# Transformer pair with batch attention and experts: the pace of the last groups' scatters, and the place of one ranking product

## The chip, the cores and the metric

The kernel runs on one core of one Trainium2 chip, as one launch. The metric is device time in microseconds (us) for the whole program, the median of several runs. The core's engines are TensorE (PE, with its weight loads shown apart as PEld), VectorE (DVE), ScalarE (ACT), GpSimd (POOL) and SyncE (SP, which issues DMAs); each works through its own queue in order, and the queues are tied together by semaphores.

## The reference

Two layers run over x of shape (16, 512, 128). Each layer normalises, mixes and adds back twice. Layer 0 has causal linear attention and a token-shift FFN; layer 1 has retention and then what this change touches: an attention over the **batch** axis and a mixture of eight experts.

```python
def _mha(x, Wqkv, bqkv, Wo, bo):         # x is (S, B, 128): every attention is over only 16 rows
    S, B, _ = x.shape
    qkv = x @ Wqkv.T + bqkv
    q, k, v = jnp.split(qkv, 3, axis=-1)
    to_heads = lambda t: t.reshape(S, B, H, hd).transpose(1, 2, 0, 3)
    q, k, v = (to_heads(q), to_heads(k), to_heads(v))
    att = jax.nn.softmax(jnp.einsum('bhqd,bhkd->bhqk', q, k) * (1.0 / np.sqrt(hd)), axis=-1)
    o = jnp.einsum('bhqk,bhkd->bhqd', att, v).transpose(2, 0, 1, 3).reshape(S, B, D)
    return o @ Wo.T + bo
def _moe(x, Wg, W1, b1, W2, b2):
    idx = jnp.argmax(xf @ Wg.T, axis=-1)
    for e in range(E):
        m = (idx == e)[:, None].astype(xf.dtype)
        h = jax.nn.relu(xf @ W1[e] + b1[e])
        out = out + m * (h @ W2[e] + b2[e])
y = _layer_norm(x + _mha(x, ...), g1, be1)
z = _layer_norm(y + _moe(y, ...), g2, be2)
```

Each of the 8192 tokens goes to one expert only, so the kernel sorts tokens by expert in a DRAM buffer `ys` and computes each expert's rows once.

## The kernel before

The program is a chain of blocks, each ended by a barrier over all engines. The last two matter here. `attend_and_route` computes the batch attention, the router's logits and each token's place in `ys`, and scatters the tokens there. `run_experts` reads `ys` in 71 slots of 128 rows, applies the expert of each slot and scatters the result to the output. It cannot begin before the barrier at the end of `attend_and_route` (the `with nc.Block()` whose exits are charged to line 1651).

`attend_and_route` handles G = 16 groups of four 128-token tiles as a software pipeline. `run` walks s from -4 to 20, and each engine has a step function that does its part for several groups: `pe_step`, `act_step`, `vec_step`, `pool_step`, `sp_step`. In step s, for a group in the range 0 to 15:

- TensorE: scores(s), q/k/v of group s+2, values(s-1) (`pe_values`, L1388), the transpose of group s+3, and the output product out(s-1) (`pe_out`, L1405, which raises the semaphore `w_ps`). Each operation waits for the operands that ScalarE, VectorE or a DMA make.
- VectorE: vec_u(s-2) (L1414, residual into the row buffer `S`), logits and statistics of it, the maximum and shift of scores(s) (L1334, L1339), the rest of the softmax and a transpose (L1369) whose result SP copies into the tile `ax` by four DMAs (L1377); values(s) waits for these.
- Routing goes by units: pairs of groups for units 0 to 6 (groups 0 and 1, ..., 12 and 13), then group 14 alone (unit 7) and group 15 alone (unit 8). For a unit r, `vec_choose(r)` (L1459 to L1468) picks each token's expert and ends in a prefix scan; `pe_rank(r)` (L1478, L1479) counts tokens ahead of each one; `vec_dest(r)` (L1485 to L1494) turns this into row numbers in `dest`, by a cast on L1492, and carries the counts on to the next unit.
- GpSimd: `pool_row(g, t)` (L1512) scatters tile t of group g into `ys` by an indirect DMA of 128 rows. Group s-5 is scattered in step s. Row t = 0 waits until the unit's `dest` and the group's row contents are there.

What spaces the scatters: up to step 11, GpSimd's own arithmetic for later groups stands between them. From step 12 on (s >= G - 4) that arithmetic has run out but for one addition, and `pool_step` holds the rows of a group back by hand: row 1 after scores(s) (`s_ps`), row 2 after values(s-1) (`o_ps`), row 3 after out(s-1) (`w_ps`), each capped at the last group that exists. After the last scatter, `clear_semaphores` clears unused semaphores, and GpSimd waits until all scatters have landed (`rows_out`). VectorE meanwhile computes the slot tables from the last unit, and SP and ScalarE write eight padding tiles into `ys` (`write_pad`, L1499).

Of the kernel before, what the change touches and what calls it, by code (L numbers as in the profile page):

```python
# [1127 lines left out]
def attend_and_route(nc, A, K, slot_row, expert):  # L1128
# [6 lines left out]
    G = NT // 4  # L1135
    left = sorted(set(nc.released_uncleared_semaphores) - set(K.cleared))
    UG, RG, VG = 7, 6, 5
    with ExitStack() as ctx:
# [380 lines left out]
        def there(g):  # L1519
            return 0 <= g < G  # L1520


        def pe_step(pe, s):
            if there(s):
                pe_scores(pe, s)
            if there(s + 2):
                pe_qk(pe, s + 2)
                pe_v(pe, s + 2)
            if there(s - 1):
                pe_values(pe, s - 1)  # L1530
            if there(s + 3):
                pe_T(pe, s + 3)
            if there(s - 1):
                pe_out(pe, s - 1)
            if even(s - 4) and s < G:
                pe_rank(pe, (s - 4) // 2)
            if G - 1 <= s <= G + 1:
                pe_rank(pe, s - 9)
# [38 lines left out]
        def vec_step(v, s, link):  # L1577

            if there(s - 2):
                vec_u(v, s - 2)  # L1580
                vec_logits(v, s - 2)
                vec_stats(v, s - 2)
            if even(s - 5) and s < G:
                vec_dest(v, link, (s - 5) // 2)
            if there(s):
                vec_max(v, s)
                vec_shift(v, s)
            if there(s - 2):
                vec_var(v, s - 2)
            x_stats(v, s)  # L1590
            if s in PARTS:
                v.wait_ge(stats, 4 * (PARTS[s][2] - 2))
                vec_x_var(v, *part_of(s))
            if even(s - 4) and s < G:
                vec_choose(v, link, (s - 4) // 2)
            if there(s):
                vec_total(v, s)
                vec_reciprocal(v, s)
                vec_probs(v, s)
                vec_transpose(v, s)  # L1600
            if s in PARTS:
                vec_x_offset(v, *part_of(s))
            if s == G or s == G + 1:
                vec_dest(v, link, s - 10)
            if G - 1 <= s <= G + 1:
                vec_choose(v, link, s - 9)
            if s == G + 1:
                vec_dest(v, link, s - 9)

        def pool_step(pool, s):  # L1610

            if s >= G - 4:
                if there(s - 5):
                    pool_row(pool, s - 5, 0)
                pool.wait_ge(s_ps, min(s + 1, G))
                if there(s + 3):
                    pool_xb(pool, s + 3)
                if there(s - 5):
                    pool_row(pool, s - 5, 1)
                    pool.wait_ge(o_ps, min(s, G))  # L1620
                    pool_row(pool, s - 5, 2)
                    pool.wait_ge(w_ps, min(s, G - 1))
                    pool_row(pool, s - 5, 3)
                return
            if there(s - 5):
                pool_row(pool, s - 5, 0)
            if there(s + 4):
                pool_scale(pool, s + 4)
            if there(s - 5):
                pool_row(pool, s - 5, 1)  # L1630
            if there(s + 4):
                pool_h(pool, s + 4)
            if there(s - 5):
                pool_row(pool, s - 5, 2)
            if there(s + 3):
                pool_xb(pool, s + 3)
            if there(s - 5):
                pool_row(pool, s - 5, 3)

        def even(g):  # L1640

            return there(g) and g % 2 == 0
# [478 lines left out]
```

## Time and profile before

| | before |
|---|---|
| runs shown, us | 1056.25 (median), 1048.0, 1058.28 |
| profiled execution, us | 1047.97 |
| its span, first to last instruction | 1046.2 |
| its mean granted TensorE clock | 0.934 |
| busy over the span: PE, DVE, ACT, POOL | 82%, 83%, 60%, 69% |
| `attend_and_route` | about 684 to 874.4 us of the span |
| `run_experts` | 874.4 to 1046.1 us |

The table comes from the page of the profile and from the start and end times of instructions in the trace. All times in the views below are in us from the start of the span. A timeline row gives start, duration, engine, line, operation, tiles written and read, count, and in brackets how long the engine was idle ahead of it and what released it. Several like instructions in a row are merged. Matmul ends are modelled.

### The profile page before, as it was taken

The numbers are of one execution on the slowest core, as the hardware profiler recorded it, in microseconds if no ns is written. First come the engines' busy times: TensorE is split into PE (matmuls) and PEld (weight loads), VectorE is DVE, ScalarE is ACT, GpSimd is POOL, SyncE is SP. The second block draws the span as 40 slices with busy tenths as digits, with TensorE's granted clock in tenths as the row PEclk, the third lists the DMA queues.
The fourth block names the chain that finished last, engine by engine and source line by source line (L and its number), as shares of the span: only waits on it lengthen the run. The fifth ranks groups of instructions, "written<-read, shape, count | busy, mean of one in ns | idle before, by whom it ended". The sixth has DMA issues, their size and how long they took to land. (4 is left out here: it accounts for less than half of the span.)

```text
span 1046.2 us, 25423 instructions
## 1 busy us (share of the span) xinstructions
PE 860.2 (82%) x5240; PEld 618.0 (59%) x5240; DVE 867.7 (83%) x2853; ACT 631.7 (60%) x1636; POOL 721.6 (69%) x626
## 2 busy tenths in 40 slices
PE   5799999999968867989898989558888732999993
PEld 5466666666636644555555555335555532999993
DVE  5589999999976976989898989778899761899995
ACT  2555555555438956676767675467665202999992
POOL 4488888888852218999999999665598461355554
PEclk9899999999989989999999999869999755999997
DMA  9520000000000000000000000254576664544420
GB/s 245 164 69 1 0 0 0 0 0 0 1 4 1 0 1 1 11 20 10 20 10 20 10 20 10 67 153 110 158 213 205 186 221 124 146 129 132 133 65 20
DMA packets 64935, 70.11 MB, mean 67 GB/s; under 512 B 8965, under 2 KB 52178, under 8 KB 64740
## 3 DMA queue, kind: packets, MB, share of 16 engines
q1 hardware_dynamic: 50612, 47.20, 16.2%
q0 software_dynamic: 6368, 16.89, 4.7%
q10 hardware_dynamic: 7872, 5.08, 1.8%
q8 instruction: 32, 0.52, 0.2%
q14 instruction: 51, 0.42, 0.1%
HBM read 32.32 MB, written 24.50 MB: 54 GB/s over the span
## 5 line engine op out<-in xcount | busy, mean ns | idle before, releaser
L473 PE MATMUL a_pS<-a_kv,utri 128*128 128x360 f32 (+3 forms) x768 | 264.9, 481 | 19.4 <-POOL a_kv L464 9.7
L464 POOL TENSOR_TENSOR a_kv<-a_qk,a_vv 128x1152 f32<-128x1152 f32 (+1 forms) x128 | 264.2, 2065 | 12.6 <-DVE a_qk L438 12.6
L473 PEld LDWEIGHTS a_pS<-a_kv,utri 128*128 128x128 f32 x768 | 136.3, 191 | 100.8 <-issue 25.3
L569 POOL TENSOR_TENSOR a_tt<-a_tt 128x576 f32<-128x576 f32 (+1 forms) x128 | 156.9, 1226 | 49.9 <-DVE a_tt L553 46.0
L553 DVE TENSOR_TENSOR a_tt<-a_pS,a_qk 128x360 f32<-128x360 f32 (+3 forms) x384 | 181.0, 526 | 11.3 <-PE a_pS L473 8.3
L1930 POOL DMA_INDIRECT out_dram<-x_o,x_place x71 | 69.1, 973 | 78.6 <-DVE x_o L1917 75.9
L581 DVE TENSOR_REDUCE a_nd<-a_tt 128x144 f32<-128x720 f32 (+3 forms) x128 | 104.5, 816 | 0.0
L519 ACT ACTIVATE a_tt<-a_pI 128x144 f32<-128x144 f32 (+1 forms) x96 | 40.1, 417 | 105.5 <-PE a_pI L481 105.4
L512 PEld LDWEIGHTS a_pO<-wgate,a_yT 128*128 128x128 f32 x256 | 44.8, 193 | 75.2 <-issue 36.6
L1512 POOL DMA_INDIRECT ys<-m_S,m_dest x64 | 63.0, 984 | 36.8 <-issue 12.3
L512 PE MATMUL a_pO<-wgate,a_yT 128*128 (+1 forms) x256 | 54.7, 296 | 30.8 <-POOL a_yT L543 22.6
L1868 PE MATMUL x_pZ<-w,x_hT 128*128 x568 | 76.9, 279 | 1.4 <-issue 1.3
L1819 ACT ACTIVATE x_w<-w 128x644 f32 x71 | 52.4, 741 | 31.3 <-PEq L1651 26.3
L1868 PEld LDWEIGHTS x_pZ<-w,x_hT 128*128 128x128 f32 x568 | 69.9, 194 | 2.1 <-issue 1.9
L410 ACT ACTIVATE a_vv<-a_pQ 128x128 f32<-128x128 f32 x122 | 33.8, 277 | 55.3 <-PE a_pQ L401 53.4
L372 ACT ACTIVATE a_xn<-X,nmr,rstd 128x128 f32 (+1 forms) x128 | 60.9, 485 | 2.0 <-DVE nmr L275 1.8
L287 DVE BATCH_NORM_STATS2 bn<-X 128x6 f32<-128x128 f32 (+1 forms) x256 | 57.4, 278 | 1.1 <-DMA X<-xs 0.9
L401 PE MATMUL a_pQ<-W,a_hT 128*128 128x384 f32 x122 | 51.5, 504 | 4.2 <-ACT a_hT L388 2.7
L456 POOL TENSOR_TENSOR a_qk<-a_ra,a_rb 128x256 f32<-128x256 f32 x64 | 47.0, 735 | 8.7 <-DVE a_rb L449 8.7
L401 PE MATMUL a_pQ<-wqkv,a_hT 128*128 128x384 f32 x122 | 50.3, 494 | 1.5 <-ACT a_hT L388 1.5
L481 PEld LDWEIGHTS a_pI<-a_R,a_qT 128*128 128x128 f32 x192 | 34.4, 189 | 28.4 <-ACT a_qT L525 11.3
L1850 ACT ACTIVATE x_hT<-x_pA,x_w 128x128 f32<-128x128 f32 x142 | 43.9, 362 | 9.4 <-PE x_pB L1842 9.4
(298 smaller groups left out, 2192.8 us busy)
## 6 DMA issues: line engine op xcount, KB each, us to landing
x_yl<-ys SPq DMA_DIRECT2D x71, 193.5 KB, 2.4
X<-xs SPq DMA_DIRECT2D x16, 256.0 KB, 5.4
kx<-m_kc SPq DMA_DIRECT2D x64, 64.0 KB
ax<-m_pc SPq DMA_DIRECT2D x64, 64.0 KB
m_S<-X SPq DMA_DIRECT2D x16, 256.0 KB, 3.1
xs<-X SPq DMA_DIRECT2D x15, 256.0 KB
w<-in_L_ffn_W_dram SPq DMA_DIRECT2D x1, 2048.0 KB
m_S<-gw ACTq DMA_DIRECT2D x6, 256.0 KB, 3.0
```

Of the source, the lines that this page charges most:

```text
L287: v.bn_stats(K.bn[:, ds(n, 1), :].rearrange("p a f -> p (a f)"), x[:, ds(n, 1), :].rearrange("p a f -> p (a f)"))\
L372: act.activation(xn[:, t, :], tile(K.X, 4 * b + t), ACT.Identity, bias=column(K.nmr, 4 * b + t), scale=column(K.rstd, 4 * b + t)).then_inc ...
L401: pe.matmul(bank_of(b, t, start)[:, 0:3 * P], hT[:, t * P:(t + 1) * P], wqkv, start=True, stop=True).then_inc(qkv_ps, 1)
L464: pool.tensor_tensor(kv[:, t % 2, :, :, :], kk.unsqueeze(2).to_broadcast([P, H, J, D]), vv[:, t, :, :].unsqueeze(3).to_broadcast([P, H, J, ...
L473: pe.matmul(pS[c][:, 0:(h1 - h0) * SC], K.utri[:, :], flat[:, h0 * SC:h1 * SC], start=True, stop=True).then_inc(u_done, 1)
L512: pe.matmul(pO[:, 0:P], yT[:, :], tile(K.wgate[:, 0 if layer == 0 else 2, :, :], b), start=True, stop=True).then_inc(proj_ps, 1)
L553: v.tensor_tensor(tt[:, t % 2, h0:h1, :, 0:D], pS[c][:, 0:(h1 - h0) * SC].rearrange("p (h j i) -> p h j i", i=D, j=J), q[:, h0:h1, :].unsq ...
L569: pool.tensor_tensor(tt[:, t % 2, :, :, D // 2:D], tt[:, t % 2, :, :, D // 2:D], tt[:, t % 2, :, :, 0:D // 2], ALU.add).then_inc(half_done, 1)
L581: v.tensor_reduce(nd[:, t % 2, :, :], tt[:, t % 2, :, :, D // 2:rows], AX.X, ALU.add).then_inc(red_done, 1)
L1512: pool.indirect_dma_start(out=A["ys"], out_offset=bass.IndirectOffsetOnAxis(ap=dest[:, g // 2 % 2, at:at + 1], axis=0), in_=S[:, 4 * (g % ...
L1868: mm = pe.matmul(pZ[j % 2][:, 0:P], hT[:, j % 2, c * P:(c + 1) * P], K.w2[:, ds(e, 1), c, :].rearrange("p a f -> p (a f)"), start=(c == 0) ...
L1930: pool.indirect_dma_start(out=token_rows, out_offset=bass.IndirectOffsetOnAxis(ap=place[:, j:j + 1], axis=0), in_=o[:, j % 4, :], in_offse ...
```

## The change

Three edits, all in the steps of `attend_and_route`:

1. TensorE: `pe_rank(5)` (groups 10 and 11) stands in front of `pe_out(13)` in step 14, instead of behind it.
2. VectorE: `vec_dest(5)` stands at the end of step 14, instead of after the statistics of group 13 in step 15.
3. GpSimd: from step 15 on (groups 10 to 15) the rows of a group are scattered one after the other; the waits for `s_ps`, `o_ps` and `w_ps` between them are gone. Steps 12 to 14 (groups 7 to 9) keep theirs, without the caps that no longer bite.

```diff
@@ pe_step @@
             if there(s + 3):
                 pe_T(pe, s + 3)
+            if s == G - 2:
+                pe_rank(pe, (s - 4) // 2)
             if there(s - 1):
                 pe_out(pe, s - 1)
-            if even(s - 4) and s < G:
+            if even(s - 4) and s < G - 2:
                 pe_rank(pe, (s - 4) // 2)
@@ vec_step @@
-            if even(s - 5) and s < G:
+            if even(s - 5) and s < G - 1:
                 vec_dest(v, link, (s - 5) // 2)
...
-            if s == G or s == G + 1:
-                vec_dest(v, link, s - 10)
+            if G - 2 <= s <= G + 1 and s != G - 1:
+                vec_dest(v, link, 5 if s == G - 2 else s - 10)
@@ pool_step @@
+            if s >= G - 1:
+                for t in range(4):
+                    if there(s - 5):
+                        pool_row(pool, s - 5, t)
+                return
             if s >= G - 4:
                 if there(s - 5):
                     pool_row(pool, s - 5, 0)
-                pool.wait_ge(s_ps, min(s + 1, G))
+                pool.wait_ge(s_ps, s + 1)
                 if there(s + 3):
                     pool_xb(pool, s + 3)
                 if there(s - 5):
                     pool_row(pool, s - 5, 1)
-                    pool.wait_ge(o_ps, min(s, G))
+                    pool.wait_ge(o_ps, s)
                     pool_row(pool, s - 5, 2)
-                    pool.wait_ge(w_ps, min(s, G - 1))
+                    pool.wait_ge(w_ps, s)
                     pool_row(pool, s - 5, 3)
                 return
```

On TensorE, in step 14 and at the start of step 15: L1388 is values(13), L1405 is out(13), L1478 and L1479 are rank(5), and the two rows behind them are scores(15).

```order
 L1388 MATMUL m_pO<-ax,m_v 32x128 x16
-L1405 MATMUL m_rows_ps<-wo,m_oT 128x136 x4
 L1478 MATMUL m_rows_ps<-m_hot,m_before 128x64
 L1479 MATMUL m_rows_ps<-m_upto,m_ones 128x64
+L1405 MATMUL m_rows_ps<-wo,m_oT 128x136 x4
 L1320 MATMUL m_pS<-m_mask 128x512
 L1327 MATMUL m_pS<-kx,m_qT 32x128 x16
```

The ranking product of unit 5 now runs between values(13) and out(13), and scores(15) follow out(13) directly.

On VectorE, at the turn from step 14 to step 15: L1369 is the softmax's transpose of group 14, L1485 to L1494 are dest(5), L1414 to L1430 are the residual, logits and statistics of group 13, and L1334 is the maximum over scores(15).

```order
 L1369 STREAM_TRANSPOSE m_pc<-m_pn 128x512
-L1414 TENSOR_TENSOR m_S<-m_rows_ps,m_U 128x4x128
-L1421 TENSOR_TENSOR m_raw<-m_rows_ps,m_v 128x32
-L1429 BN_STATS m_ubn<-m_S 128x6 x4
-L1430 COPY m_S<-m_ids 128x4
 L1485 TENSOR_TENSOR m_pick<-m_rows_ps,m_hot 128x64
 L1488 TENSOR_REDUCE m_posf<-m_pick 128x8
 L1492 CAST m_dest<-m_posf 128x8
 L1494 COPY m_hot<-m_upto 128x8
+L1414 TENSOR_TENSOR m_S<-m_rows_ps,m_U 128x4x128
+L1421 TENSOR_TENSOR m_raw<-m_rows_ps,m_v 128x32
+L1429 BN_STATS m_ubn<-m_S 128x6 x4
+L1430 COPY m_S<-m_ids 128x4
 L1334 TENSOR_REDUCE m_mx<-m_pS 128x16
```

The four instructions of dest(5) now come ahead of the four rows of group 13 that wait for out(13).

On GpSimd, groups 10 and 11. Semaphores are reused and show under the names of earlier owners: s_tab is `s_ps`, a0_x_done is `o_ps`, a0_sd_done is `w_ps`; the long lists are the conditions of a group's row 0.

```order
 L1512 DMA ys<-m_S,m_dest 67456x387 [waits a0_var_done,a0_rope_b,a0_rstd,a0_kv_ready,a0_qkv_ps,a0_u_done,a0_red_done]
-L1512 DMA ys<-m_S,m_dest 67456x387 [waits s_tab]
-L1512 DMA ys<-m_S,m_dest 67456x387 [waits a0_x_done]
-L1512 DMA ys<-m_S,m_dest 67456x387 [waits a0_sd_done]
+L1512 DMA ys<-m_S,m_dest 67456x387 x3
 L1512 DMA ys<-m_S,m_dest 67456x387 [waits a0_var_done,a0_rope_b,a0_std,a0_kv_ready,a0_hT_ready,a0_u_done,a0_red_done]
-L1512 DMA ys<-m_S,m_dest 67456x387 [waits s_tab]
-L1512 DMA ys<-m_S,m_dest 67456x387 [waits a0_x_done]
-L1512 DMA ys<-m_S,m_dest 67456x387 [waits a0_sd_done]
+L1512 DMA ys<-m_S,m_dest 67456x387 x3
```

The order of the scatters is the same; rows 1 to 3 of these groups, and of the four behind them, no longer wait for anything of their own.

## Rows read from the trace of the kernel before

**Rows 1.** Source view, line 1651 (block exit): ns min/median/max, first to last start us

```profile
L1651 SPq COMPARE_BRANCH  x1: 38/38/38, 863.7 to 863.7; - x1
L1651 POOLq COMPARE_BRANCH  x1: 41/41/41, 868.8 to 868.8; - x1
L1651 POOLq DRAIN  x1: 5287/5287/5287, 869.0 to 869.0; - x1
```

**Rows 2.** Source view, line 1934 (exit of the last block)

```profile
L1934 POOLq DRAIN  x1: 5841/5841/5841, 1040.1 to 1040.1; - x1
```

**Rows 3.** Timeline of GpSimd, the last scatter of the last block

```profile
1037.67 0.97 POOL L1930 DMA_INDIRECT out_dram<-x_o,x_place  x1 [0.30 <-issue]
```

**Rows 4.** Timeline of GpSimd from 830 to 866 us, scatters into ys

```profile
830.35 0.97 POOL L1512 DMA_INDIRECT ys<-m_S,m_dest  x1 [1.99 <-DVE m_S L1414]
832.68 0.97 POOL L1512 DMA_INDIRECT ys<-m_S,m_dest  x1 [1.36 <-DVE m_dest L1492]
...
836.55 0.97 POOL L1512 DMA_INDIRECT ys<-m_S,m_dest  x1 [1.62 <-PE m_pO L1388]
...
846.64 0.97 POOL L1512 DMA_INDIRECT ys<-m_S,m_dest  x1 [0.30 <-issue]
...
865.80 0.97 POOL L1512 DMA_INDIRECT ys<-m_S,m_dest  x1 [0.30 <-issue]
```

**Rows 5.** Timeline of TensorE from 808 to 837 us, steps 11 to 15

```profile
808.98 1.08 PE L1388 MATMUL m_pO<-ax,m_v 128*32 128x128 f32 x32 [2.85 <-DMA ax<-m_pc]
...
825.48 1.08 PE L1388 MATMUL m_pO<-ax,m_v 128*32 128x128 f32 x32 [3.17 <-DMA ax<-m_pc]
827.37 2.18 PE L1405 MATMUL m_rows_ps<-wo,m_oT 128*128 128x136 f32 x8 [0.81 <-ACT m_oT L1396]
829.34 0.52 PE L1478 MATMUL m_rows_ps<-m_hot,m_before 128*128 128x64 f32 x2
...
830.22 0.60 PE L1320 MATMUL m_pS<-m_mask 2*128 2x512 bf16 x1
...
833.78 1.94 PE L1388 MATMUL m_pO<-ax,m_v 128*32 128x128 f32 x32 [1.09 <-DMA ax<-m_pc]
836.52 2.18 PE L1405 MATMUL m_rows_ps<-wo,m_oT 128*128 128x136 f32 x8 [0.81 <-ACT m_oT L1396]
```

**Rows 6.** Timeline of VectorE from 801 to 853 us

```profile
801.40 0.71 DVE L1369 STREAM_TRANSPOSE m_pc<-m_pn 128x512 f32<-128x512 f32 x1
...
826.16 0.31 DVE L1468 TENSOR_TENSOR_SCAN m_upto<-m_reset,m_hot 128x72 f32<-128x72 f32 x1
...
828.09 0.71 DVE L1369 STREAM_TRANSPOSE m_pc<-m_pn 128x512 f32<-128x512 f32 x1
829.58 0.69 DVE L1414 TENSOR_TENSOR m_S<-m_rows_ps,m_U 128x512 f32<-128x512 f32 x1 [0.78 <-PE m_rows_ps L1405]
...
831.16 0.26 DVE L1485 TENSOR_TENSOR m_pick<-m_rows_ps,m_hot 128x64 f32<-128x64 f32 x1
...
831.71 0.17 DVE L1492 CAST m_dest<-m_posf 128x8 uint32<-128x8 f32 x1
...
832.83 0.69 DVE L1334 TENSOR_REDUCE m_mx<-m_pS 128x16 f32<-128x512 f32 x1 [0.87 <-PE m_pS L1327]
...
839.48 0.67 DVE L1414 TENSOR_TENSOR m_S<-m_rows_ps,m_U 128x512 f32<-128x512 f32 x1
...
841.90 0.17 DVE L1492 CAST m_dest<-m_posf 128x8 uint32<-128x8 f32 x1
...
852.74 0.17 DVE L1492 CAST m_dest<-m_posf 128x4 uint32<-128x4 f32 x1
```

**Rows 7.** Windows view: busy PE, PEld, DVE, ACT, POOL (count); granted clock, DMA share, GB/s

```profile
845.00:855.00 10.00, 3.70 (x16) 3.23 (x15) 6.48 (x36) 0.51 (x2) 7.56 (x9) 0.50 0.42 157
855.00:865.00 10.00, 0.00 (x0) 0.00 (x0) 3.48 (x7) 0.00 (x0) 7.56 (x9) 0.50 0.93 310
```

**Rows 8.** Part 6 of the page, DMA issues: count, KB of each

```profile
ax<-m_pc SPq DMA_DIRECT2D x64, 64.0 KB
```

## Prediction

> **What bounds the kernel now.** The change touches one block, so I first ask what ends that block. The sources view of its exit line shows when each queue got there. SP, which waits for the padding tiles, is through at 863.7; GpSimd gets there last, at 868.8, and then spends 5.29 us in a DRAIN that ends at 874.3 [rows 1]. All other engines pass the barrier right after that and the next block starts. So GpSimd alone decides when the experts begin.
>
> Does that DRAIN hang on the last scatter or on its own start? The last block ends the same way and gives a second sample. There the last scatter starts at 1037.67 and the DRAIN runs from 1040.1 to 1045.9, 8.3 us after that start [rows 2, 3]. Here the last scatter starts at 865.80 and the DRAIN ends 8.5 us later [rows 1, 4]. The two DRAINs differ by 0.55 us but the sums by 0.2 us. I take 8.4 us from the start of the last scatter to the barrier as fixed: what the last scatter gains, the kernel gains, since the experts behind the barrier are not changed.
>
> Now the timeline of GpSimd, read backward from 865.80. From 846.64 on there are sixteen scatters (groups 12 to 15), each 0.97 us long with 0.30 us between them; 15 steps take 19.16 us, 1.277 each [rows 4]. That is the engine's own pace, and it holds although VectorE works beside it until about 852.9 and DMA engines are 0.93 busy from 855 to 865 [rows 6, 7]. In front of these the engine idles: between 830.35 and 846.64 lie 16.29 us for nine scatter starts that would need 9 x 1.277 = 11.49. The 4.80 us of difference sit in waits like the 1.62 for values(14) and the 1.36 for dest(5) [rows 4]. This is the most the change can free, if nothing else holds group 12.
>
> **The change, part by part.**
>
> *Rank(5) in front of out(13).* values(13) start at 825.48 and take 1.08, so TensorE is free at 826.56; out(13) waits for ScalarE until 827.37, an idle of 0.81 [rows 5]. What rank(5) needs, the scan, is done at 826.16 + 0.31 = 826.47 [rows 6], so it fits there. Its cost behind out(13) was 829.34 to 830.22, 0.88 us at the lower clock level (granted clock 0.50, that is 1.2 GHz, as in [rows 7]; values(14) take 1.94 against 1.08 for values(13) [rows 5]). In the 0.81 gap it delays out(13) by 0 to 0.1 us: I take nothing; the cover is ScalarE's eviction, and without it the edit would only swap 0.88 us. If the scan came later than some 826.5, out(13) and all behind it would wait. Scores(15) now start at 829.34 instead of 830.22, 0.88 earlier.
>
> *Dest(5) at the end of step 14.* VectorE ends the transpose of group 14 at 828.80 and idles 0.78 until out(13) at 829.58 [rows 6]. Dest(5) took from 831.16 to 831.96 (the maximum at 832.83 less its idle of 0.87), 0.80 us. It fills that idle; 0.02 us stick out, which I count as nothing. Group 13's four rows then run from 829.6 to 831.2 and the maximum over scores(15) can start at 831.95, 0.88 earlier, if scores(15) do. Dest(5)'s cast ends near 829.4 instead of 831.88; the scatter behind that cast came 0.80 us after its end (832.68), so row 0 of group 10 could go at 830.2, and waits only for its turn.
>
> *The waits on GpSimd.* Row 3 of group 9 keeps its wait for out(13), so 830.35 stays. From there eight scatters of groups 10 and 11 follow at 1.277: 831.63 to 840.57, and group 12 could start at 841.84. What is late next is dest(6). Its cast ended at 842.07 [rows 6]; with 0.80 behind it that gives 842.87. But its chain moves too. It hangs on VectorE's residual of group 14, which began at 839.48 behind choose(6) without idle. 0.88 earlier would be 838.60, yet out(14), held by the arrival of `ax` for values(14) at 833.78, still starts at 836.52 and takes 2.18, to 838.70 [rows 5]. So the residual starts at 838.7, 0.75 earlier, the cast ends at 841.32 and row 0 of group 12 goes at 842.12. Fifteen steps later the last scatter starts at 861.28, against 865.80: 4.5 us gained. Group 15's row 0 comes at 857.4, while dest(8) was there at 852.91 [rows 6], so 3.7 us of slack remain behind the 0.80.
>
> *The unknown: `ax`.* More scatters now run while the copies of probabilities for values(14) and (15) are in flight. The trace of before does not show these copies under unspaced scatters. From the end of the transpose to the first product, group 14 took 4.98 us (828.80 to 833.78), with two scatters started in between; group 10 took 6.87 us (802.11 to 808.98) amid other transfers [rows 4 to 6]. From below the change costs nothing, since only one scatter more starts in the flight of `ax`(14); from above it costs the difference, 1.9 us. Each us moves the residual of group 14, and the last scatter with it. I take 0.3 us, near the lower end, because two scatters out of three were there before. For `ax`(15) the 3.7 us of slack cover even the 1.9.
>
> The Trainium skill speaks against this change here: its page "DMA: Bandwidth & Descriptors", section "Queues, rings and completion order", says that a DMA engine takes turns, packet by packet, between the queues that have work, so a scatter in flight takes turns away from the copy. By the rule, four copies of 64 KB [rows 8], 0.26 MB or 0.85 us at the 310 GB/s of [rows 7], would take up to twice that, an estimate; the sum would be 4.5 - 0.85 = 3.7 us instead of 4.2, and no row isolates it.
>
> **Sum**: 4.5 - 0.3 = 4.2 us; bounds 2.6 (with 1.9) and 4.5. The profiled execution would go from 1047.97 to 1043.8. It is one of the short ones: the runs shown are 1048.0, 1056.25 and 1058.28, so two times lie near 1048 and two near 1057, and nothing in the profile says which a run will be. The mean of the four is 1052.6; less 4.2 gives 1048.4, which is my number. From the median alone it would be 1052.0.
>
> **Rivals.**
> - *The copies are crowded.* `ax`(14) lands 1.9 us late, gain 2.6: 1050.0. For it: group 10's 6.87 us. Against it: then three streams ran at once, here the last q/k copies are over.
> - *DMA engines bind at the end.* From 855 to 865 they are 0.93 busy [rows 7]; perhaps earlier scatters only queue before the padding tiles. In the 10 us before they are at 0.42, so the 3.5 scatters that move up (0.2 MB each, 0.7 MB) do their work there; 0.7 MB less at 310 GB/s is 2.3 us less from the crowded stretch. If that were all, 1050.3. Against it: SP had its tiles landed at 863.7 while GpSimd arrived at 868.8, a margin of 5.1 us [rows 1]. If SP's arrival did not move at all, the gain could still be the full 4.5.
> - *Nothing moves.* The barrier would hang on something beside the last scatter, or an unseen limit paces the scatters: 1052.6. Against it: the two sums of 8.3 and 8.5.
> - *Slower.* The mechanism is `ax`(14) again, at a price no row shows. Break-even is a copy 4.5 us late, 9.5 us in all against 4.98. If it took three times 4.98 us, 10 us late, the residual of group 14 would come 9.2 us later than before and dest(6) with it; the kernel would take 5.5 us more, 1058.1. For over 1% it must be 15 us late.
> - *More than forecast.* TensorE, with its gap filled, stays at the higher level: scores(15) take 0.86 less. Then only GpSimd's own pace binds (841.84), 0.3 more than 4.5: 1047.8.
>
> **How the numbers follow.** Chances: my forecast with a gain between 3.3 and 4.7, 0.60; crowded copies 0.16; DMA engines 0.08; nothing moves 0.08; slower than before 0.04; more than forecast 0.04. The range: the short runs less the full gain give 1043.5, with 1.5 of scatter 1042; the long ones, 1058.28 less 2.6, give 1055.7, and with nothing moved a little over: 1057. About 1% is what a measurement of this kernel can tell from no change, given times that lie 10 us apart. The gain is 0.4%, so within 1% is likely, 0.78. That a median of three falls among the short runs after the change, when it fell among the long ones before (1043.8 against 1056.25 is 1.2%), gets 0.18 for faster; 0.04 is for slower, from the fourth rival and the same chance turned round.
>
> **What would show it.** Right: the last scatter of the block starts near 861 and the DRAIN ends 8.4 us later, near 869.9; no idle but 0.30 between scatters from 830.35 to 840.6, a wait under 0.5 us in front of group 12; dest(5)'s cast ends near 829.4; the maximum over scores(15) starts near 831.95; SP arrives by 864. Wrong: values(14) start over 1 us later behind their transpose than 4.98 us, out(13) starts after 827.6, scatters take longer than 0.97 us, or the DRAIN grows by what the scatters gained. Then the term with its row above is the one that failed.

## The result, and the profile after

The changed kernel took 1052.39 us (median of 22 runs, 1049.21 to 1059.03); the kernel before, timed beside it, 1049.09 (22 runs, 1046.81 to 1058.28). The ratio is 1.0031, with a 95% interval of 1.0016 to 1.0047: slower by 0.3%, where 0.4% faster was forecast. The same change, timed again in later sets of runs, gained 0.3% in two of them; why is the main question below.

| | before | after |
|---|---|---|
| profiled execution, us | 1047.97 | 1056.49 |
| its span | 1046.2 | 1054.7 |
| its mean granted TensorE clock | 0.934 | 0.931 |
| first scatter of group 9 | 823.07 | 826.45 |
| last scatter of the block | 865.80 | 875.10 |
| GpSimd's DRAIN at the block's exit starts | 869.0 | 878.6 |
| from there to the end of the span | 177.2 | 176.1 |

Only part of the 9.3 us by which the last scatter is later belongs to the change. The first scatter of group 9 stands in front of every edit and is already 3.38 us later. So I measure from it to the last scatter, since the edits lie in that stretch: 42.73 us before, 48.65 after, 5.9 us more. This is the row of before that the sum starts from:

```profile
823.07 0.97 POOL L1512 DMA_INDIRECT ys<-m_S,m_dest  x1 [0.30 <-issue]
```

The timeline of GpSimd in the changed kernel, against [rows 4]:

```profile
826.45 0.97 POOL L1512 DMA_INDIRECT ys<-m_S,m_dest  x1 [0.30 <-issue]
...
836.10 0.97 POOL L1512 DMA_INDIRECT ys<-m_S,m_dest  x1 [4.75 <-PE m_rows_ps L1405]
837.37 0.98 POOL L1512 DMA_INDIRECT ys<-m_S,m_dest  x1 [0.30 <-issue]
...
846.33 0.97 POOL L1512 DMA_INDIRECT ys<-m_S,m_dest  x1 [0.30 <-issue]
855.84 0.97 POOL L1512 DMA_INDIRECT ys<-m_S,m_dest  x1 [8.53 <-DVE m_dest L1492]
...
875.10 0.98 POOL L1512 DMA_INDIRECT ys<-m_S,m_dest  x1 [0.30 <-issue]
```

From 836.10 to 846.33 the spacing is gone, nine starts at 1.277 to 1.28 us each, as forecast. What was forecast as a wait under 0.5 us in front of group 12 is 8.53 us, for dest(6). The source view of the exit (line 1659 here), against [rows 1]:

```profile
L1659 POOLq COMPARE_BRANCH  x1: 41/41/41, 878.4 to 878.4; - x1
L1659 POOLq DRAIN  x1: 5287/5287/5287, 878.6 to 878.6; - x1
L1659 SPq COMPARE_BRANCH  x1: 38/38/38, 880.5 to 880.5; - x1
```

SP, which was 5.1 us ahead of GpSimd, is now through 2.1 us behind it, but the DRAIN still ends last, at 883.9. Its length is the same to the nanosecond.

Why is dest(6) late? First the timeline of TensorE, against [rows 5]:

```profile
832.26 0.69 PE L1478 MATMUL m_rows_ps<-m_hot,m_before 128*128 128x64 f32 x2 [3.39 <-DVE m_upto L1468]
832.75 0.63 PE L1479 MATMUL m_rows_ps<-m_upto,m_ones 128*128 128x64 f32 x2
833.17 2.13 PE L1405 MATMUL m_rows_ps<-wo,m_oT 128*128 128x136 f32 x8
835.23 0.60 PE L1320 MATMUL m_pS<-m_mask 2*128 2x512 bf16 x1
835.76 1.94 PE L1327 MATMUL m_pS<-kx,m_qT 128*32 128x128 f32 x32
839.26 1.92 PE L1388 MATMUL m_pO<-ax,m_v 128*32 128x128 f32 x26 [1.56 <-DMA ax<-m_pc]
841.82 0.66 PE L1388 MATMUL m_pO<-ax,m_v 128*32 128x128 f32 x5 [0.64 <-issue]
843.28 0.39 PE L1388 MATMUL m_pO<-ax,m_v 128*32 128x128 f32 x1 [0.80 <-issue]
850.19 2.18 PE L1405 MATMUL m_rows_ps<-wo,m_oT 128*128 128x136 f32 x8 [6.52 <-ACT m_oT L1396]
```

Then VectorE, against [rows 6]:

```profile
831.90 0.31 DVE L1468 TENSOR_TENSOR_SCAN m_upto<-m_reset,m_hot 128x72 f32<-128x72 f32 x1
...
843.27 0.69 DVE L1334 TENSOR_REDUCE m_mx<-m_pS 128x16 f32<-128x512 f32 x1 [6.08 <-DMA blk<-in_k_blk_dram]
...
852.41 0.69 DVE L1414 TENSOR_TENSOR m_S<-m_rows_ps,m_U 128x512 f32<-128x512 f32 x1 [2.42 <-PE m_rows_ps L1405]
...
854.87 0.17 DVE L1492 CAST m_dest<-m_posf 128x8 uint32<-128x8 f32 x1
```

And the eviction of values(14) on ScalarE:

```profile
849.45 0.69 ACT L1396 ACTIVATE m_oT<-m_pO,cols 128x512 f32<-128x512 f32 x1 [3.67 <-remote]
```

Read them as pairs of a producer's end and its reader's start. The record of scores(15) ends at 835.76 + 1.94 = 837.70. VectorE has been idle since 837.19 and starts the maximum over them at 843.27, 5.57 us later (the releaser named there is a load long done; the instruction waits for the semaphore of the scores alone, which rises at 843.24 by the semaphore events in the trace). The record of values(14) ends at 843.67, with gaps of 0.64 and 0.80 us inside the product that no row of before has, and ScalarE starts to evict it at 849.45, 5.8 us later and idle for the last 3.67 of them; the product's semaphore rises at 849.43. In the profile of before the same two steps took 0.13 us (scores(15) end at 832.70, the maximum starts at 832.83) and 0.06 (835.72 and 835.78). So both 32-column products, the scores and the values, are issued in time by their records, and their completion reaches the readers 5.6 and 5.8 us late. (The ends of matmul records are modelled, so the products themselves may have run long, or a finished product was reported late. One row speaks for the first: the last matmul of values(14) starts at 843.28, 0.04 us after the semaphore of scores(15), and in the second profile of the changed kernel at 842.39 against 842.35. TensorE seems held as well, and not the report alone. That is not shown.) Then the chain runs at its usual pace: out(14) 850.19, residual 852.41, cast of dest(6) 854.87 + 0.17, row 0 of group 12 at 855.84, and fifteen steps later, at 875.10, the last scatter. In what follows I call this a **late product**: the record of the product has ended, its reader starts over 1 us later, and the reader was idle just before that. A reader that was busy until its start says nothing about the product.

Windows view of the changed kernel, against [rows 7]:

```profile
845.00:855.00 10.00, 4.79 (x44) 4.13 (x44) 6.79 (x28) 1.95 (x6) 1.95 (x2) 0.50 0.46 140
855.00:865.00 10.00, 4.64 (x18) 4.17 (x18) 7.06 (x40) 1.19 (x3) 7.03 (x8) 0.50 0.32 119
```

TensorE is at the same lower level (0.50) as before; the clock doesn't explain 5 us. VectorE has 7.06 us of work behind 855, against 3.48 before.

### The profile page after: what moved, and what is told of

The parts are those of the page before. It is cut to its first block and busy times, and to the rows that moved or that the text cites. A ratio compares the mean times of both kernels' runs of the same rounds, so it can differ in the third digit from the quotient of the medians.

```text
span 1054.7 us, 25423 instructions
## 1 busy us (share of the span) xinstructions
PE 860.9 (82%) x5240; PEld 617.1 (59%) x5240; DVE 867.1 (82%) x2853; ACT 631.3 (60%) x1636; POOL 722.4 (68%) x626
```

## The experiments

Five sets of runs, each with its own runs of the kernel before. Its medians were 1045.55, 1048.39, 1045.04, 1046.33 and 1045.71 us; in the first timing above it was 1049.09. "From group 9" is the time from group 9's first scatter to the last scatter, in the profile of that run: 42.73 for before, 48.65 for the changed kernel.

**The floor.** The kernel before was timed twice more, against its own runs.

> The kernel before itself, for its profile on this chip. Theory P: products at most 0.6 us late. Theory Q: on a chip where the changed kernel shows 5 to 9 us, this one shows 1 to 3 us in steps 13 to 15; where it shows none, the changed kernel shows none.

> The kernel before itself, for its profile in this call. Theory Q: products of steps 13 to 15 over 1.5 us late only if the changed kernel shows 5 us or more; from the fourth call, where the changed kernel gained, 1.6 us at most is seen here.

Measured: 1044.57 us, 0.9981 (0.9962 to 0.9999), and 1045.45 us, 1.0000 (0.998 to 1.002); from group 9: 41.9 and 42.06. So 0.2% can appear from nothing, even with an interval that just excludes 1, and the profile of before in front of the prediction (42.73) is at the long end of its kind.

**Set 1: which part loses?** The GpSimd edit alone:

```diff
@@ pool_step of the kernel before @@
+            if s >= G - 1:
+                for t in range(4):
+                    if there(s - 5):
+                        pool_row(pool, s - 5, t)
+                return
```

> The kernel before with the GpSimd edit alone: scatters of groups 10 to 15 without spacing, ranking and dest(5) where they were. Theory A (the back-to-back scatters make TensorE finish scores(15) and values(14) late, by some 5 us each in the profile after): slower than before by 0.2 to 0.5%, and the maximum over scores(15) starts more than 1 us behind the last product of scores(15). Theory B (the loss is the ranking product in front of out(13), which waits there for a late scan): 0.3% faster, since eight scatters lose their waits. Theory C (the profiled execution was only an unlucky one and the parts do nothing): within 0.1%.

Measured: 1042.60 us, 0.9976 (0.9962 to 0.9991); from group 9 38.96. Faster by some 2.5 us, where the whole change was forecast to gain 4.2, and no late product.

The move of rank(5) and dest(5) alone (the first two edits of the change, GpSimd as before):

> The kernel before with the TensorE and VectorE edits alone, all spacing of the scatters kept. Theory A: between the same and 0.1% faster, the maximum over scores(15) starts within 0.3 us of the last product. Theory B: slower than before by 0.2 to 0.5%, with out(13) starting over 1 us after ScalarE has made its operand. Theory C: within 0.1%.

Measured: 1046.48, 1.0012 (0.9998 to 1.0026); from group 9 41.3. Nothing to gain, perhaps a little to lose.

The GpSimd edit one step later (`if s >= G:`, so group 10 keeps its waits), without and with that move:

> The kernel before with the spacing taken away only from step 16 on (groups 11 to 15); group 10, which is scattered while scores(15) and values(14) run, keeps its three waits. Theory A: the same or up to 0.1% faster (0.8 us of one wait), no late products. If instead any unspaced scatter beside values(15) hurts, it is slower by 0.2% or more.

> The changed kernel with the three waits of group 10 put back (ranking and dest(5) moved, groups 11 to 15 unspaced). Theory A: 0.1 to 0.2% faster than before, about 1 to 1.5 us: 0.75 from the earlier chain and 0.8 from one wait. Theory B: slower by 0.2% or more, like the changed kernel.

Measured: 1044.13, 0.9983 (0.9965 to 1.0001), from group 9 42.5; and 1046.50, 1.0001 (0.9985 to 1.0016), 42.85. By the profiles, group 10's spacing is thus most of what the edit frees; the timings, 0.9976 and 0.9983, don't tell the two apart. After this set the move looked guilty, but the change itself had not been run beside its parts.

**Set 2: the change again, and what of it makes products late.**

> The changed kernel once more, on the chip that also runs the next three. Theory A (back-to-back scatters that start early, because dest(5) is early, make TensorE finish scores(15) and values(14) late; each part alone is harmless): 0.2 to 0.4% slower than before, products of scores(15) or values(14) finish over 1 us late. Theory B (ranking in front of out(13) costs 1 to 2 us, the free scatters give 2.5 us back; the two add up): 0.05 to 0.2% faster than before, and out(13) starts behind the scan by at least 0.7 us.

Measured: 1050.05, 1.0014 (0.9992 to 1.0035); from group 9 48.8. The interval holds 1, so this timing alone doesn't show a loss. The profile repeats the first one: scores(15) 5.55 us late, values(14) 5.78.

With group 10 held until scores(15) are done, so that no unspaced scatter is beside them:

```diff
             if s >= G - 1:
+                if s == G - 1:
+                    pool.wait_ge(s_ps, G)
                 for t in range(4):
```

> The changed kernel with one wait put back: row 0 of group 10 waits until scores(15) are done. Theory A: faster than the changed kernel by 0.2% or more, since no scatter of the unspaced run overlaps scores(15). Theory B: the same as the changed kernel or up to 0.1% slower.

Measured: 1052.07, 1.0032 (1.0012 to 1.0052); from group 9 48.3. Timelines of TensorE, ScalarE and GpSimd:

```profile
835.34 1.19 PE L1388 MATMUL m_pO<-ax,m_v 128*32 128x128 f32 x32 [2.12 <-DMA ax<-m_pc]
```
```profile
845.55 0.69 ACT L1396 ACTIVATE m_oT<-m_pO,cols 128x512 f32<-128x512 f32 x1 [9.52 <-remote]
```
```profile
834.18 0.97 POOL L1512 DMA_INDIRECT ys<-m_S,m_dest  x1 [1.28 <-PE m_pS L1327]
...
843.12 0.97 POOL L1512 DMA_INDIRECT ys<-m_S,m_dest  x1 [0.30 <-issue]
851.92 0.97 POOL L1512 DMA_INDIRECT ys<-m_S,m_dest  x1 [7.83 <-DVE m_dest L1492]
```

Scores(15) come in time now, and values(14), whose record ends at 836.53 without a gap, are 9.02 us late. Their reader is released 2.4 us after the last scatter of group 11 starts.

With dest(5) back behind group 13's statistics, so that group 10 starts later by another way:

```diff
@@ vec_step of the changed kernel @@
-            if even(s - 5) and s < G - 1:
+            if even(s - 5) and s < G:
...
-            if G - 2 <= s <= G + 1 and s != G - 1:
-                vec_dest(v, link, 5 if s == G - 2 else s - 10)
+            if s == G or s == G + 1:
+                vec_dest(v, link, s - 10)
```

> The changed kernel with dest(5) put back behind group 13's statistics; ranking stays in front of out(13), scatters unspaced from step 15. Theory A: like the gate, 0.2% or more faster than the changed kernel, because group 10's scatters start 1.5 to 3 us later. Theory B: within 0.1% of the changed kernel, as the hold of out(13) by the scan is the same.

Measured: 1052.86, 1.0043 (1.0020 to 1.0067); from group 9 49.3. Timelines of TensorE and ScalarE:

```profile
833.34 1.08 PE L1388 MATMUL m_pO<-ax,m_v 128*32 128x128 f32 x32 [2.00 <-DMA ax<-m_pc]
```
```profile
843.48 0.69 ACT L1396 ACTIVATE m_oT<-m_pO,cols 128x512 f32<-128x512 f32 x1 [9.44 <-remote]
```

The same: scores(15) in time, values(14) 9.06 us late, again until 2.5 us after group 11's last scatter started (841.02). The large late product is not tied to scores or to where dest(5) stands. In this set it was whichever 32-column product was in work while the eight scatters of groups 10 and 11 ran without a pause.

Is it the bytes? The kernel before, with its scatters spaced, and eight plain copies of 256 KB more from ScalarE's queue in step 14 (the computation is unchanged):

```diff
+            if s == G - 2:
+                for i in range(8):
+                    act.dma_start(A["zz"][P * i:P * i + P, :],
+                        K.w2[:, i, :, :].rearrange("p c f -> p (c f)")).then_inc(zz_out, 16)
```

> The kernel before, with eight plain DMAs of 256 KB each from an SBUF weight tile to an unused DRAM buffer, issued by ScalarE in step 14, ahead of scores(15). It asks if DMA load beside them delays TensorE's products, whatever issues it. Theory A in the form that bytes do it: scores(15) or values(14) finish over 2 us behind their last product. In the form that GpSimd's indirect DMAs do it: within 0.6 us as in the profile before, only the copies for values(14) land later, by up to 3 us.

Measured: one time, 1050.57 us. TensorE's and ScalarE's timelines:

```profile
838.01 1.94 PE L1389 MATMUL m_pO<-ax,m_v 128*32 128x128 f32 x32 [4.87 <-DMA ax<-m_pc]
...
843.61 1.94 PE L1389 MATMUL m_pO<-ax,m_v 128*32 128x128 f32 x32
```
```profile
840.01 0.69 ACT L1397 ACTIVATE m_oT<-m_pO,cols 128x512 f32<-128x512 f32 x1 [3.83 <-PE m_pO L1389]
...
848.11 0.69 ACT L1397 ACTIVATE m_oT<-m_pO,cols 128x512 f32<-128x512 f32 x1 [2.55 <-remote]
```

With 279 GB/s in flight from 830 to 840 (DMA engines 0.84 busy) values(14) are done as soon as they are computed, although they start 6.65 us behind the transpose's end, against 4.98, waiting for `ax`; values(15) are 2.56 us late. So bytes delay the copies more than the products. They may contribute to a late product; in this one execution they made none of 9 us.

This profile shows more. Up to step 14 its program is that of the kernel before, and yet scores(14), ahead of the added copies and of any unspaced scatter, are 1.29 us late by the rows of TensorE and VectorE:

```profile
821.92 1.94 PE L1328 MATMUL m_pS<-kx,m_qT 128*32 128x128 f32 x32
```
```profile
825.15 0.69 DVE L1335 TENSOR_REDUCE m_mx<-m_pS 128x16 f32<-128x512 f32 x1 [1.93 <-PE m_pS L1328]
```

**Set 3: is the ranking to blame, or the data of the scatters?** The changed kernel with rank(5) behind out(13) again:

```diff
@@ pe_step of the changed kernel @@
-            if s == G - 2:
-                pe_rank(pe, (s - 4) // 2)
             if there(s - 1):
                 pe_out(pe, s - 1)
-            if even(s - 4) and s < G - 2:
+            if even(s - 4) and s < G:
                 pe_rank(pe, (s - 4) // 2)
```

> The changed kernel with the ranking of unit 5 put back behind out(13); dest(5) stays at the end of step 14, so VectorE waits there for it, scatters unspaced from step 15. If ranking in front of out(13) is the part that turns the gain of the free scatters into a loss: faster than before by 0.1 to 0.3%, from the last start of group 9's first scatter to the last scatter 39 to 41 us, no product over 3 us late. If dest(5) early (group 10's scatters beside scores(15)) is the part: slower by 0.1 to 0.4%, 48 us from that scatter to the last, scores(15) or values(14) 5 to 9 us late.

> The GpSimd edit alone once more, on the chip of the other runs of this call. If the first result holds: faster than before by 0.1 to 0.4%, about 39 us from group 9's first scatter to the last (before 42.7, changed 48.7), values(14) finish within 0.5 us of their last product. If late products are a matter of chance that any unspaced scatters bring: 5 to 9 us late in this profile, and not faster.

Measured: 1042.48, 0.9976 (0.9958 to 0.9993), from group 9 38.7; and the GpSimd edit alone again, 1041.98, 0.9966 (0.9950 to 0.9982), 38.2. Neither has a late product. Together with set 2 this seemed to settle it: rank(5) in front of out(13) makes the products late. It did not, as the next set shows.

The changed kernel with the eight scatters of groups 10 and 11 issued in their places with a bound of 0, so that their rows are dropped, and the real eight behind them:

```diff
-                        pool_row(pool, s - 5, t)
+                        pool_row(pool, s - 5, t, drop=s - 5 in (10, 11))
+                if s - 5 == 11:
+                    for g in (10, 11):
+                        for t in range(4):
+                            pool_row(pool, g, t)
```

> The changed kernel, but the eight unspaced scatters of groups 10 and 11 run with a bound of 0, so that GpSimd does all its work and hardly any row is moved; the real eight follow behind them (some 10 us more in all). If the late products come from the data in flight (DMA engines, SBUF or DRAM traffic): scores(15) and values(14) finish within 0.5 us. If they come from GpSimd's own work for the scatters: 5 to 9 us late as in the changed kernel.

Measured: one time, 1052.13 us, with some 10 us of scatters added (the dropped ones don't wait for dest(5) either). No late product: values(14) run from 832.46 to 834.39 and are evicted from 834.46 on. By itself this would say that the data of the scatters is needed. But no kernel of this set had a late product, so it tells nothing. A variant meant to space these eight scatters by GpSimd work, without a wait on TensorE, gave no result; whether spacing by itself keeps the products in time stays untested.

**Set 4: the change and its parts side by side.**

> The changed kernel, now on one chip with its parts. Theory P (the ranking in front of out(13) holds TensorE until the scan, costs 1 to 2 us, and together with unspaced scatters brings the late products): slower than before by 0.1 to 0.4%, and slower than the free scatters alone by 0.4 to 0.7%; scores(15) or values(14) 5 to 9 us late. Theory Q (the late products belong to the chip: the whole kernel, without the GpSimd edit too, has them on some chips and not on others): on a chip where the kernel before shows products at most 0.6 us late, the changed kernel shows none either and is 0 to 0.2% faster than before.

> The GpSimd edit alone on the same chip. Theory P: 0.2 to 0.4% faster than before whatever the chip, no late products. Theory Q: on a chip with late products (over 1 us in the profile of the kernel before) it has them too, 5 to 9 us, and is slower than before; on a chip without, 0.2 to 0.4% faster.

> Ranking and dest(5) moved, scatters spaced, same chip. Theory P: 0.05 to 0.2% slower than before (out(13) starts behind the scan and the ranking, 1 to 2 us after its operand is there); no late products. Theory Q says the same of the hold; its late products would come on a chip that has them, up to 2.6 us in step 14.

Measured: the change 1043.03, **0.9973** (0.9952 to 0.9994), from group 9 39.2; the GpSimd edit alone 1043.37, 0.9968 (0.9948 to 0.9987), 40.0; the move alone 1045.63, 0.9992 (0.9974 to 1.0010), 42.35. The change, with rank(5) in front and eight scatters in a row, has no late product and is faster.

**Set 5: once more.**

> The changed kernel once more beside its GpSimd edit alone and the kernel before. Theory Q (a condition of chip and time decides: where DMA traffic makes TensorE's 32-column products finish late, the unspaced scatters lose; elsewhere they gain): if the kernel before takes about 1045 us and its profile shows no product over 1.5 us late, this is 0.1 to 0.4% faster; if it takes 1048 or more and shows 1 to 3 us late, this is 0.1 to 0.4% slower with 5 to 9 us late. Theory P (the combination with the moved ranking loses on its own): slower in both cases; the last run has already spoken against it.

> The GpSimd edit alone. Theory Q: the same sign as the changed kernel in this call, within 0.2% of it; where products are late, this one has late products too. If the moved ranking is needed for the late products: faster than before by 0.2 to 0.4% even where the changed kernel is slower.

Measured: the change 1043.10, **0.9976** (0.9959 to 0.9993), from group 9 38.5; the GpSimd edit alone 1044.75, 0.9992 (0.9976 to 1.0008), 39.25.

### What the sets say together

| | late products in the profile | change against before |
|---|---|---|
| first timing (before: 1049.09) | scores(15) 5.6, values(14) 5.8 | +0.31% |
| set 2 (before: 1048.39) | in the change and both its variants, 5.6 to 9.1 | +0.14% |
| sets 4 and 5 (before: 1046.33, 1045.71) | none | -0.27%, -0.24% |

*Shown:* the same program gains 2.5 to 2.8 us by its ratio where no product is late, and costs 1.5 to 3.3 where its profile has late ones. Each of these is close to the 0.2% that two timings of one kernel can lie apart; the stretch from group 9 in the profiles, 38.5 and 39.2 us against 41.9 to 42.7 before, and 48.65 and 48.8 with late products, is the clearer evidence. Late products are there ahead of every edit too: scores(14) are 1.3 to 2.6 us late in five profiles, the changed kernel twice, e6, e7 and e8, and at most 0.5 in the fifteen others. All four profiles of set 2 are among the five, e8 with the spaced scatters of the kernel before. In the first timing and set 2 the kernel before took 1048 to 1049 us instead of 1045 to 1046. So there is a condition outside the change, and in set 2 the large late product lay beside the unspaced scatters in both variants as well. It is not the chip by itself: sets 2 and 4 are on record with the same chip number, 24 minutes apart.

*Not shown:* what that condition is, by what way a completion is held, and how many executions it touches. A profile is one execution, and those of the changed kernel with late products were long ones (1056.49 and 1055.28 us, medians 1052.39 and 1050.05), so 5.9 us in the profile and 1.5 to 3.3 in the timing need not conflict. The profile of the kernel before in front of the prediction, a short execution of 1047.97, has no late product, although its three runs are among the 22 of the first timing. Nor whether the moved ranking is needed for the loss. The GpSimd edit alone was timed in sets 1, 3, 4 and 5, and none of them had late products in any kernel; it was never timed in the sets that had.

## Why the prediction was wrong

**The step that failed in this timing: dest(6) comes when `ax` lets it.** The sum let the chain from values(14) over out(14) and the residual to dest(6) be late by one term alone, the copies into `ax`, at 0.3 us with an upper bound of 1.9, and put the time from a product's end to its reader at nothing. In the profile of the changed kernel `ax` cost nothing, and values(14) reached ScalarE 5.8 us after their record's end; GpSimd waited 8.53 us for dest(6), and the stretch from group 9 grew by 5.9 us instead of shrinking by 4.2. Why the product was late stays open. The steps below would have left a gain of some 2.5 us.

**The pace of the scatters: right.** Groups 10 and 11 go at 1.277 us a start, the wait for out(13) in front of them stays, scatters take 0.97 us, and the GpSimd edit by itself gains 0.08 to 0.34% in its four timings, the move of ranking and dest(5) nothing in its two (1.0012 and 0.9992).

The other steps are best read where no product is late. This is the profile of the changed kernel in set 5; GpSimd:

```profile
820.95 0.97 POOL L1512 DMA_INDIRECT ys<-m_S,m_dest  x1 [0.30 <-issue]
...
827.62 0.97 POOL L1512 DMA_INDIRECT ys<-m_S,m_dest  x1 [3.13 <-PE m_rows_ps L1405]
...
840.21 0.97 POOL L1512 DMA_INDIRECT ys<-m_S,m_dest  x1 [1.39 <-DVE m_dest L1492]
...
859.45 0.97 POOL L1512 DMA_INDIRECT ys<-m_S,m_dest  x1 [0.30 <-issue]
```

TensorE, VectorE and ScalarE in step 14:

```profile
824.40 0.43 PE L1478 MATMUL m_rows_ps<-m_hot,m_before 128*128 128x64 f32 x2 [2.21 <-DVE m_upto L1468]
824.67 0.39 PE L1479 MATMUL m_rows_ps<-m_upto,m_ones 128*128 128x64 f32 x2
824.90 1.92 PE L1405 MATMUL m_rows_ps<-wo,m_oT 128*128 128x136 f32 x8
...
831.86 1.92 PE L1388 MATMUL m_pO<-ax,m_v 128*32 128x128 f32 x32 [2.92 <-DMA ax<-m_pc]
```
```profile
824.04 0.31 DVE L1468 TENSOR_TENSOR_SCAN m_upto<-m_reset,m_hot 128x72 f32<-128x72 f32 x1
...
825.98 0.71 DVE L1369 STREAM_TRANSPOSE m_pc<-m_pn 128x512 f32<-128x512 f32 x1
```
```profile
822.46 0.67 ACT L1396 ACTIVATE m_oT<-m_pO,cols 128x512 f32<-128x512 f32 x1
```

And the kernel before in the same set (its first scatter of group 9, its last, and the exit), with the exit of the changed kernel below:

```profile
822.89 0.97 POOL L1512 DMA_INDIRECT ys<-m_S,m_dest  x1 [0.30 <-issue]
...
864.95 0.97 POOL L1512 DMA_INDIRECT ys<-m_S,m_dest  x1 [0.30 <-issue]
```
```profile
L1651 POOLq COMPARE_BRANCH  x1: 41/41/41, 868.1 to 868.1; - x1
```
```profile
L1659 POOLq COMPARE_BRANCH  x1: 41/41/41, 863.6 to 863.6; - x1
```

**"Rank(5) in front of out(13)" at nothing: wrong.** The prediction took the idle of 0.81 us and the scan's end at 826.47 from one profile, in which values(13) had waited 3.17 us for `ax` [rows 5]. Its own condition was "if the scan came later than some 826.5, out(13) and all behind it would wait". In set 5 the operand of out(13) is ready at 823.13, the scan ends at 824.35, 1.22 us later, and out(13) starts at 824.90, 1.77 us after it could; in the first profile of the changed kernel 833.17 against 830.99, 2.2 us. Over the profiles without a late product, the scan ends 0.7 to 1.2 us behind the operand in eleven (e1 to e4, e9 to e11, e13, e16 to e18), within 0.3 us of it in two (e15, e19), and well ahead in two (e14 by 1.41, and before by 0.85): the prediction rested on the rarer order. What the move gives back, an earlier scores(15), is hardly a gain either: with ranking in its old place TensorE waits there for VectorE's probabilities of group 14 in seven of ten profiles, 0.18 to 0.94 us. The GpSimd edit alone shows it in set 1:

```profile
826.27 0.60 PE L1320 MATMUL m_pS<-m_mask 2*128 2x512 bf16 x1 [0.94 <-DVE m_pn L1362]
```

**"0.75 earlier" for dest(6): wrong, by most of it.** From group 9's first scatter to the one that waits for dest(6) the changed kernel in set 5 has 840.21 - 820.95 = 19.26 us. The cast itself comes 18.29 us after that scatter, and 18.59 in e13. The sum had it at 841.32 - 823.07 = 18.25, so the time was right; what was wrong is that it took the move to bring it there. Without the move the cast comes at 18.83, 17.96 and 18.14 in the three profiles of before, and at 18.34, 17.25, 19.42 and 17.84 in the four of the GpSimd edit alone. The wait in front of group 12 is 1.39 us (0.48 in e13), where the forecast had under 0.5.

**"8.4 us from the last scatter to the barrier as fixed": wrong, by about 1 us.** From the start of the last scatter to GpSimd's arrival at the exit the set 5 profiles have 868.1 - 864.95 = 3.15 us before and 863.6 - 859.45 = 4.15 after. The DRAIN behind it takes its 5.29 us in either. What goes with the difference is how busy the DMA engines are in the 3 us ahead of the last scatter (windows view; the share is the last number but one), after first, then before:

```profile
856.45:859.45 3.00, 0.00 (x0) 0.00 (x0) 0.00 (x0) 0.00 (x0) 2.08 (x4) 0.50 1.05 308
```
```profile
861.95:864.95 3.00, 0.00 (x0) 0.00 (x0) 0.00 (x0) 0.00 (x0) 2.08 (x4) 0.50 0.69 241
```

In the seven profiles with an arrival 3.6 to 4.7 us behind the last scatter (e1, e9, e10, e13, e14, e17, e18) this share is 1.00 to 1.09; in the thirteen others it is 0.36 to 0.89, and the arrival comes after 2.9 to 3.3 us. The likely reason is that SP is through at 861.9 after and at 862.8 before: the padding tiles come at nearly the same time as before, and the earlier last scatters run into them. The changed kernel with late products, whose last scatters are late again, has 3.1 to 3.3. This was the rival "DMA engines bind at the end" in small: it left a gain of 2.3 out of 4.2, a cost of 1.9, and costs about 1.

**"I take 0.3 us" for `ax`: right.** From the end of the transpose to values(14) there are 831.86 - 826.69 = 5.2 us in set 5 against 4.98 in [rows 5, 6] and 4.7 in the kernel before of set 5: 0.2 to 0.5. In the first profile, where products were late, 839.26 - 834.55 = 4.7: the late products are not `ax`.

**The sum where nothing is late.** In set 5 the last scatter moves by 42.06 - 38.50 = 3.56 us relative to group 9, not 4.5 - 0.3; the exit takes 1.0 of it, 2.56 are left, and the timing says 1045.71 - 1043.10 = 2.6. Two things make up the difference to 4.2: the exit, left at zero, costs 1.0, and the profile that the sum started from is a long one of its kind. The sum put the stretch at 42.73 - 4.2 = 38.5 us and set 5 has 38.50, which is luck in part, as set 4 has 39.2; but the kernel before usually takes 41.9 to 42.1.

**The slower rival named the wrong thing.** It had the right shape: something that dest(6) hangs on comes more than 4.5 us late. But it priced only the copies into `ax`, because they were the one thing in the trace that waits for DMA, and took the completion of the products that use them for granted. The chance of 0.04 was for that one mechanism, not for a release on TensorE that comes late.

**Number and range.** 1048.4 was built as the mean of four times less 4.2; with 22 runs the kernel before is 1049.09, so the base of 1052.6 was 3.5 us too high. Against the forecast the result is 4.0 us off; with the right base it would have been 7.5. The luck of the base hid nearly half. The time of 1052.39 lies inside 1042 to 1057, and within 1% was right, as was all that any set gave.

## What to carry to other kernels

Before an instruction is moved into an idle slot, read in several profiles which of the two operands comes first; one profile of a pipeline that sometimes waits 3 us for a copy shows one order of several. Take as fixed only what has been seen under the load that the change will bring: GpSimd reached the exit 2.9 to 3.3 us after the last scatter where the DMA engines had room, and 3.6 to 4.7 where they had none. Take the starting point of a sum from more than one profile. And where the effect is a few tenths of a percent, run the unchanged kernel as its own rival, and the change in more than one set beside its parts: two sets here would each have told a clear story (the change loses; the ranking is to blame), and two later ones contradict both.

## What the runs showed of the hardware

- A product's record can end and its semaphore rise 5.5 to 9.1 us later. Only scores(15) and values(14), 32-column products (L1327, L1388), did so, in the first timing and set 2, while indirect scatters of 128 rows went out one every 1.277 us; the readers of values(14) were released 2.4 to 3.1 us after the last of the eight had started. In the same profiles scores(14) were 1.7 to 2.6 us late before any unspaced scatter, and 1.29 in a kernel whose scatters were spaced (e8). In sets 1, 3, 4 and 5 scores(14) and (15) and values(14), where their reader was idle, started it within 0.15 us, beside the same unspaced scatters and from the same program in sets 4 and 5. Cause open. The Trainium skill, page "SBUF — State Buffer", section "SBUF: two separate sides", holds that DMA and compute engines use separate ports and cannot slow each other. By that rule the traffic of the scatters could not reach a product through SBUF; the runs show the large late products beside unspaced scatters in some sets only, and don't show a way between them.
- The DRAIN that GpSimd runs at the end of `attend_and_route` took 5287 ns in nineteen of the twenty profiles (6037 in e11, the one with eight scatters more), whether the last scatter had started 3.1 or 4.9 us before it.
- GpSimd reached the exit, behind its wait for all scatters, 2.9 to 3.3 us after the start of the last one where the DMA engines were 0.36 to 0.89 busy in the 3 us ahead of it, and 3.6 to 4.7 us where they were 1.00 to 1.09 busy.
- Beside eight plain copies of 256 KB the copies into `ax` took 6.65 us from the transpose to the product instead of 4.98; one product was 2.56 us late (one execution, in set 2).
- The same kernel against itself: 0.9981 and 1.0000.
